# Six scatter groups in place of seven, a denser scatter of the first two, and zero rows written late, in an attention and mixture-of-experts kernel

## What is computed

```python
def reference(x, condB_zX, condB_zY, condB_zR, ...):
    ...
        logits = hn2 @ router_w.T
        rp = jax.nn.softmax(logits, axis=-1)
        topw, topi = jax.lax.top_k(rp, K)
        gates = jnp.sum(jax.nn.one_hot(topi, E, dtype=hn2.dtype) * topw[..., None], axis=1)
        hmid = jax.nn.gelu(jnp.einsum('th,ehf->tef', hn2, w1), approximate=False)
        y = jnp.einsum('tef,efh->th', hmid * gates[:, :, None], w2)
        return x1 + y.reshape(s, b, h)
    x = x + _L0_ffn_ref(_L0_cond_ref(x, ...), ...)
    return x
```

## The kernel before, in words

| iteration | slots before | slots after | steps scattered before | steps scattered after |
|---|---|---|---|---|
| 10, 11, 12 | none | none | 0 1, 2 3, 4 | none |
| 13 | -1 | none | none | 0 1 2 3 |
| 14 | none | none | 5 6 | 4 5 6 7 |
| 15 | none | -1, 0, 1 | 7 8 | none |
| 16 | 0, 1 | 2, 3, 4 | none | none |
| 17 | 2, 3 | 5 | none | 8 9 10 11 |
| 18 | 4, 5 | 6, 7 | 9 10 | none |
| 19 | 6, 7 | 8, 9 | 11 12 | none |
| 20, 21 | 8, 9 | 10, 11 | none | none, 12 13 |
| 22, 23, 24 | 10 to 15 | 12 to 17 | none, 13 14, 15 16 | 14 15, none, none |
| 25 | none | 18 | 17 | none |
| 26 | 16, 17 | 19, 20 | none | 16 17 |
| 27 | 18, 19 | 21 | none | 18 19 |
| 28 | 20, 21 | none | 18 19 | 20 |
| 29, 30 | 22 to 25 | 22 to 25 | 20 21, 22 | none |
| 31 to 34 | 26 to 30 | 26 to 30 | 23 to 26 in 32 and 33 | 21 to 25 |

## Time and profile before

### The profile page before, as it was taken

One profiled execution on the slowest core, in us unless ns is written; L12 is line 12 of the kernel. 1 busy time (PEld: TensorE's weight loads), 2 busy tenths in 40 slices (PEclk: granted clock), 3 DMA queues, 4 the chain that ended last, 5 costly groups with the idle time before them and its releaser, 6 DMA issues. The chain is left out here.

```text
span 723.5 us, 10160 instructions
## 1 busy us (share of the span) xinstructions
PE 585.2 (81%) x2640; PEld 405.8 (56%) x2640; DVE 434.1 (60%) x1028; ACT 349.0 (48%) x814; POOL 461.3 (64%) x562
## 2 busy tenths in 40 slices
PE   2567786764567969769999699999699999999992
PEld 1334454442346646546666466766477676676761
DVE  1256679974999998755895699989844000111110
ACT  4334443322433645527766456666257555444440
POOL 5787678688668565675778874584475854343432
PEclk9779997876888989889999699999899999999997
DMA  4377854233111321342324422243344544444332
GB/s 126 124 223 229 254 145 104 53 82 96 45 52 38 82 38 23 74 91 50 59 39 89 110 30 38 38 95 56 53 77 82 118 83 67 68 61 73 62 58 23
DMA packets 51547, 59.83 MB, mean 83 GB/s; under 512 B 7386, under 2 KB 47075, under 8 KB 51428
## 3 DMA queue, kind: packets, MB, share of 16 engines
q0 software_dynamic: 18288, 23.28, 20.2%
q1 hardware_dynamic: 33204, 35.91, 17.5%
HBM read 35.89 MB, written 27.46 MB: 88 GB/s over the span
## 5 line engine op out<-in xcount | busy, mean ns | idle before, releaser
L979 PE MATMUL b_y<-w_s,hm_hmT 128*128 x568 | 137.0, 385 | 11.8 <-ACT y L548 11.0
L446 POOL DMA_INDIRECT out_dram<-y,xin x71 | 117.9, 1660 | 34.0 <-issue 27.0
L964 PE MATMUL b_h<-w_s,xT 128*128 x284 | 134.4, 596 | 1.6 <-ACT xT L509 1.6
L979 PEld LDWEIGHTS b_y<-w_s,hm_hmT 128*128 128x128 f32 x568 | 103.5, 192 | 25.9 <-issue 14.6
L1116 PE MATMUL b_at<-ident,pv_prod 128*128 128x128 f32 x544 | 76.3, 291 | 25.8 <-DVE pv_prod L910 25.8
L681 DVE TENSOR_SCALAR y<-b_y,xin,live 128x256 f32<-128x256 f32 x24 | 13.1, 544 | 136.9 <-PE b_y L979 136.9
L910 DVE TENSOR_TENSOR pv_prod<-kv,pr 128x1024 f32<-128x1024 f32 (+2 forms) x80 | 82.6, 1074 | 19.8 <-PE b_at L1116 19.7
L844 DVE TENSOR_TENSOR qk_prod<-q,kv 128x1024 f32<-128x1024 f32 (+2 forms) x80 | 89.5, 1143 | 2.7 <-ACT kv L578 1.8
L1116 PEld LDWEIGHTS b_at<-ident,pv_prod 128*128 128x128 f32 x544 | 67.6, 154 | 30.0 <-issue 24.2
L414 POOL DMA_INDIRECT xs_d<-ring,slot_row x64 | 71.5, 1118 | 19.1 <-issue 18.2
L852 DVE TENSOR_REDUCE sc<-qk_prod 128x64 f32<-128x1024 f32 (+2 forms) x80 | 82.2, 1052 | 0.3
(11 more groups left out here) (168 smaller groups left out, 1038.1 us busy)
## 6 DMA issues: line engine op xcount, KB each, us to landing
xin<-xs_d SPq DMA_DIRECT2D x71, 132.5 KB, 2.2
w_s<-in_L_ffn_w_dram SPq DMA_DIRECT2D x16, 512.0 KB, 4.5
xp<-in_x_dram SPq DMA_DIRECT2D x32, 128.0 KB
xud<-in_x_dram SPq DMA_DIRECT2D x32, 128.0 KB
out_dram<-x POOLq DMA_DIRECT2D x32, 128.0 KB, 3.3
xud<-in_x_dram SPq DMA_DIRECT2D x32, 126.0 KB
out_dram<-y,xin POOLq DMA_INDIRECT x71, 3.9
xud<-in_x_dram SPq DMA_DIRECT2D x64, 1.0 KB
```

The lines of the kernel that those rows point to most:

```text
L446: pool.indirect_dma_start(out_rows, bass.IndirectOffsetOnAxis(ap=xin[:, j % NX, H:H + 1].bitcast(U32), axis=0), y[:, j % NY, :], None, com ...
L964: mm = pe.matmul(b_h[:, :], xT[:, k * P:(k + 1) * P], w1_s[:, bass.ds(e * (HC * F) + k * F, F)], start=(k == 0), stop=(k == HC - 1))
L979: mm = pe.matmul(b_y[:, 0:H], hmT[:, k * P:(k + 1) * P], w2_s[:, bass.ds(e * (FC * H) + k * H, H)], start=(k == 0), stop=(k == FC - 1))
```

## The change

Seven groups become six, with ends at steps 8, 12, 16, 21, 26 and 32. The first two groups are scattered four steps an iteration (one at the start, three at the end of GpSimd's iteration). `WANT` gives three slots to iterations 15 and 16, and other numbers to 17, 25, 27 and 28. The ring of normalised steps has 15 places in place of 16. The zero rows come from `xp`, which nothing uses any more after iteration 26, and are written two experts an iteration in iterations 27, 28, 30 and 31; the first tile of the last group waits for them.

```diff
--- before.py
+++ after.py
@@ -34,7 +34,7 @@
     ORDER = [(c, p) for a, b in ((0, FEW), (FEW, S)) for c in range(B // P) for p in range(a, b)]
     AGAIN = S + FEW
     KV = S + FEW
-    ENDS = (5, 9, 13, 18, 23, 27, G)
+    ENDS = (8, 12, 16, 21, 26, G)
     GROUPS = [range(a, b) for a, b in zip((0,) + ENDS, ENDS)]
     NG = len(GROUPS)
     GMAX = max(len(r) for r in GROUPS)
@@ -43,7 +43,7 @@
     TMAX = max(b - a for a, b in zip(FIRST, FIRST[1:]))
     CAP = G * P + 2 * P
     ROW = H + 1 + E
-    RING = 16
+    RING = 15
     NX = 6
     NY = 4
     SCALE = float(D) ** -0.5
@@ -135,7 +135,7 @@
         live = sb("live", [P, TMAX])
 
         xin = sb("xin", [P, NX, ROW])
-        zrow = xin[:, NX - 1, :]
+        zrow = xp[:, :, :].rearrange("p i h -> p (i h)")[:, 0:ROW]
         y = sb("y", [P, NY, H])
         xT = sb("xT", [P, HC * P])
         hm_hmT = sb("hm_hmT", [P, 2 * F])
@@ -181,16 +181,18 @@
         NPLACES = 2 + S // TP
         ROUTE = {GROUPS[r][-1] + 4: r for r in range(NG - 1)}
 
-        PER = 2
+        PER = [4, 4] + [2] * (NG - 2)
         SCATTER = {}
         for g, r in ROUTE.items():
             for i, step in enumerate(GROUPS[r]):
-                SCATTER[g + 2 + i // PER, i % PER] = step
+                SCATTER[g + 2 + i // PER[r], i % PER[r]] = step
+
+        PREFIX = (G - AHEAD - 1, G - AHEAD, G - 2, G - 1)
 
         PLACES = {0: (), 1: (0,), 2: (0, 1), 3: (0, 1, 2), 4: (0, 0, 1, 2)}
         LATER = {1: (2,), 2: (3, 4), 3: (2, 3, 4)}
 
-        WANT = [0] * 13 + [2] * 7 + [1] * 2 + [2] * 10 + [1] * 3
+        WANT = [0] * 13 + [3] * 4 + [2] * 3 + [1] * 2 + [2] * 3 + [1, 2, 1, 0] + [2] * 3 + [1] * 3
 
         def group_of(j):
             return [r for r in range(NG) if j >= FIRST[r]][-1]
@@ -300,7 +302,7 @@
                     r = group_of(j)
                     sp.wait_ge(s["tab_ready"], r + 1)
                     sp.wait_ge(scattered[r], 32 * len(GROUPS[r]))
-                if j == NX - 1:
+                if j == TAIL:
                     sp.wait_ge(s["pre_done"], 16 * E)
                 if j >= NX:
                     sp.wait_ge(*added_to(j - NX))
@@ -377,9 +379,7 @@
                 links_of.append(pool.iota(iota_w[:, :].rearrange("p (a b) -> p a b", b=2), [[16, ALL // 2 + 1], [0, 2]],
                                           base=0, channel_multiplier=0))
                 link(links_of[-1])
-                link(pool.memset(zrow, 0.0))
-                pool.tensor_copy(iota_f[:, :], iota_i[:, :])
-                pool.tensor_copy(zrow[:, H:H + 1].bitcast(I32), idt[:, 0:1]).then_inc(s["const_ready"], 1)
+                pool.tensor_copy(iota_f[:, :], iota_i[:, :]).then_inc(s["const_ready"], 1)
 
             def neighbours(g):
 
@@ -414,10 +414,13 @@
                     pool.indirect_dma_start(xs_d, bass.IndirectOffsetOnAxis(ap=slot_row[:, k, g:g + 1], axis=0),
                                             ring[:, g % RING, :], None).then_inc(scattered[r], 16)
 
-            def prefix():
-
-                pool.wait_ge(s["pre_ready"], 1)
-                for e in range(E):
+            def prefix(i):
+
+                if i == 0:
+                    link(pool.memset(zrow, 0.0))
+                    link(pool.tensor_copy(zrow[:, H:H + 1].bitcast(I32), idt[:, 0:1]))
+                    pool.wait_ge(s["pre_ready"], 1)
+                for e in (2 * i, 2 * i + 1):
                     pool.indirect_dma_start(xs_d, bass.IndirectOffsetOnAxis(ap=pre_row[:, e:e + 1], axis=0),
                                             zrow, None).then_inc(s["pre_done"], 16)
 
@@ -472,9 +475,10 @@
                     diffuse(g + AHEAD + 1)
                 for j in adds[1:]:
                     add_y(j)
-                if g == list(ROUTE)[0] + 3:
-                    prefix()
-                scatter_at(g, 1)
+                if g in PREFIX:
+                    prefix(PREFIX.index(g))
+                for n in range(1, max(PER)):
+                    scatter_at(g, n)
             left = [j - 1 for j in done_in(G + 2)] + list(range(LEFT[0] - 1, ALL))
             while left[0] < LEFT[1]:
                 add_y(left.pop(0))
```

## The result

The changed kernel takes 741.44 us (median of 4 runs, 739.84 to 741.80), the kernel before 724.88 on the same chip: the ratio is 1.0236, with a 95% interval of 1.0215 to 1.0256. The profiled execution spans 739.4 us for 723.5, so the spans differ by 15.9 and the medians by 16.6. The forecast sum was -13.1. The step from one to the other, 29 us, has to be found.

The account below looks back on a forecast made before the run. No single bound in the loop: VectorE early, GpSimd's DMAs in iteration 12, TensorE and VectorE in turns from 16; TensorE behind the loop. Window gains and costs summed to -13.1 from 724.75, so 712 us, range 701 to 725.

Parts of the forecast that it names:

- The bill of the first clump: Window 14: VectorE waits for the deviation behind eight scatter DMAs on GpSimd, +5.2 us (bounds 0, +8).
- What was priced at 5 behind it: Iteration 15: TensorE waits 5 us, cold, for the first tile at slot -1; window 15 becomes 29.0, +12.2 us.
- +1.5 in window 18 (bounds 0, +8): Window 18: GpSimd's six scatters behind two adds end 30 us into window 17; VectorE wants it at 28.3.
- Window 19, "-4.0": Iteration 19: adds due over a longer time free the result buffer TensorE waited 3.79 us for; -4.0 (bounds 0, -6).
- it keeps its length: Behind the loop: 40 slots before and after, TensorE always busy, so this part's time does not change.
- The zero rows, "+0.5 (bounds 0, +3)": Iterations 27 to 31: two zero-row DMAs each, 2.6 us, on a GpSimd with little to do; +0.5 us in all.
- 21 to 24 (+3.7) and 25 (+2.2): Windows 21 to 24 lose a routing beside full TensorE, -1.0; window 25 gains a slot and routing, +0.7 (bounds 0, +5).
- the slower one: Rival: GpSimd's queue becomes the bound from iteration 13 to 18; six windows take 147 us, total 732; chance 0.12.
- Cheap clumps: Rival: bunched scatters cost less, window 14 1 longer and window 15 needing 23.5; total 702 us; chance 0.17.
- The clock's case: Rival: iterations without slots lower TensorE's clock; half of 29 and 15 at 1.2 GHz add 4 and 7: 723; chance 0.07.

Follow-up runs that it names:

- the square: Four six-group kernels, scattered four or two steps an iteration, with three slots in some iterations or two at most: spans 739.4, 724.1, 730.0, 715.6 us.
- the last kernel: Changed kernel with all groups scattered by two, at most two slots, step 25 scattered last, four experts' zero rows each in 29 and 30: 712.65 us.

## Why the prediction was wrong

**Right.** One routing less and the zero rows out of iteration 12 gave 18.4 us in windows 9 to 13, where the sum had 20.4: without the eight DMAs alone window 12 is 9.0 us shorter, where the sum took off the whole wait of 11.31. The bill of the first clump was right in size and in place: VectorE waited 5.57 us for the deviation in window 14, where 5.2 was forecast (its own figures, 23.8 less 18.8, give 5.0). What was priced at 5 behind it, TensorE's wait for the first tile, was 8.94, and since it began earlier the window came out at 28.83 for 29.0. Windows 16, 17, 20, 27, 30 and 31 are each within 1.4.

**The step that failed is "+1.5 in window 18 (bounds 0, +8)".** It measured +13.7, beyond the upper bound. The term counted two adds, a wait for a landing and six scatters, put their end at 30 us after the start of window 17 and compared that with VectorE's need at 28.3. In the trace the last scatter ended at 284.03, 29.4 after that start, so the count was right. But an add, the neighbours and the deviations themselves come after it, up to 289.35. I had added 3.3 us for such a tail in window 14 and nothing for these 5.3; and everyone else who waits for that queue is missing. (1) Tile j is loaded when the result of tile j - 6 is added; a third slot in 15 and 16 makes this bind, since the adds come an iteration later, one landing apart. TensorE lost 3.93 us. (2) That load stands in SyncE's queue ahead of the loads of `x`; with no slot in 18 and its scatters spread, the window was still 7 us longer than before, from this and from the late adds (which of the two weighs how much wasn't separated). (3) Tile 9 is the first of its group and needs the scatters landed: 7.44 us. On top of the waits, TensorE's busy time grew by 3.8 us at the lower clock. I had written for iteration 15 that a group's first tile waits for its scatter and its load, and did not write it again for iteration 18, where it is just as true.

**Window 19, "-4.0".** It was to lose the wait for a result buffer because adds would be due over a longer time. The wait stayed, 4.07 us. Neither the third slots nor the clumps make it: it is 4.55 us with two slots and the clumps, 4.57 with two slots and no clumps, and 3.26 to 3.79 in the kernels with seven groups. Only the kernel with three slots in 17, 18 and 19 has it not, where TensorE stood 9.48 us for a tile in that window. What would remove it, no run shows.

**Behind the loop, "it keeps its length": +6.2.** I looked at the number of slots and at TensorE, which was full in the stretch read the earlier trace rows, but that began at 558.62, 22 us behind the start of window 33. Ahead of it are the last steps' deviations. Five scattered steps and the rows of 31 now stand before the last one in GpSimd's queue, where three steps did, and they have less time to pass, since window 31 without its routing takes 9.19 us for 15.87. The last deviation is ready 8.7 us after the start of window 33 (554.98), where it was 3.9 (540.53). TensorE waits 4.78 us for the step, where in the kernel before it waited 1.06:

```profile
542.09 0.44 PE L1079 MATMUL b_tr<-ident,ring 128*128 128x128 f32 x2 [1.06 <-DVE ring L672]
```

In the first 12 us of this part its granted clock is 0.78, where it was 1.00, and over the whole part it is busy for 2.3 us more. The kernel before with two experts' rows in 30 and in 31 kept its 186.9, so the rows cost here only where the queue was already late. Moving step 25 alone gave 3.0 of the 6.2 back, moving the rows of 30 and 31 alone 2.4, moving step 25 and the rows of 31 together 5.7 (192.5 to 186.8). With both moved the term "it keeps its length" holds, six steps in the last group and all.

**The zero rows, "+0.5 (bounds 0, +3)".** In the changed kernel window 28 took 2.9 more with them than with them behind the loop, but 28 and 29 together only 0.7; with the second group scattered by two, 28 and 29 together took 2.5 more. With the 2.4 that they cost behind window 32, they come to 3.1 to 4.9, at the upper bound or over it. GpSimd's share of busy time in an iteration says little of it: four experts' rows in 27 were free where 27 scattered nothing; where it scattered two steps they cost 5.2 more than two experts' there and two in 28.

**Not settled:** 21 to 24 (+3.7) and 25 (+2.2). Window 22 takes 19.36 us in the changed kernel and 16.2 to 16.4 in those with other slots in 18 or other scatters of the second group. But it also took 17.01 with step 25 moved, which touches nothing there, so that its 3 us follow from window 18 is likely and not shown. Window 25 has a routing, a slot and a clock of 0.77; it took 20.8 to 21.8 in three others with these groups (one slot in 18, two slots with and without clumps), which have two slots there. All are inside the bounds given, and no run takes it apart.

**The rivals.** The one that came nearest is the slower one, that GpSimd's queue becomes the bound from 13 to 18, at 732 us and a chance of 0.12. Its mechanism, waits for landings added to a queue in order, is what the runs show; the three-slot iterations, which it took for two adds more, are the larger half. Its size was too large there and its place too small: windows 13 to 18 took 138.0 us, where it had 147 and the forecast 126.7, and the rest of the way to 741 lies in windows 19 to 29 and behind the loop, where it added nothing. I argued against it with the deviations alone ("wanted 5 us after they can be made"), and again forgot the tiles. Cheap clumps is refuted by window 14 in both columns of the square. The clock's case did not come where it was placed: with the zero rows elsewhere, iteration 28, without a slot, took 15.27 at a clock of 0.78, 29 ran at 1.00, and 15 came out as forecast. A lower clock did cost 3.8 us in window 18 and some behind window 32, where waits had come first. That the last kernel, 712.65, meets the forecast of 712 is luck: its slots, scatters and zero rows stand elsewhere.

## What to carry to other kernels

When work is bunched in an in-order queue, list for each instruction behind it everyone who waits: the buffer that it frees, the load that stands behind another load in a second queue, and the first reader of what it writes. A wait priced once at a group's start comes again at the next group's start. And where a part "keeps its length", read its first microseconds as well as its middle; a free place in a queue is one where nothing else of that kind stands in the same iteration, not one where the engine's busy share is low. And measure the cheapest part of a change by itself: here moving the zero rows in the kernel before gave all that the best of the larger changes gave.

## What the runs showed of the hardware

An add to the output held GpSimd for 1.5 to 1.7 us (in the changed kernel up to 3.1 for some beside VectorE's products), and in a row they started 4.5 to 4.7 us apart (290.30, 294.93, 299.39), so three results took 10.6 us of the queue, from the start of the first to the end of the last, in iterations that last 17 to 20. The Trainium skill, DMA: Bandwidth & Descriptors, section Rules for kernel authors, says that an accumulating DMA reads its destination and writes it later with nothing held in between, and that one must wait for the earlier DMA's semaphore. The kernel's wait is that rule, and the 2.9 to 3.0 us of idle time ahead of each add are what it costs here.

The same elementwise instruction over 128 by 256 numbers took GpSimd 0.73 us, or 1.6, or 2.52, by what VectorE did beside it. In window 17 line 397 took 2.52 (263.05) beside a product of VectorE (line 848, from 262.73), line 398 took 0.73 (265.65) mostly beside a reduction (line 856), and line 399 took 1.60 (266.46) beside the next product. The Trainium skill, GPSIMD Engine Reference, section Key points, says that GpSimd shares its SBUF interfaces with VectorE and contends with instructions of it that have two SBUF inputs. The trace agrees: these products have two, and in window 18, while VectorE idled, the additions took 0.72 each (291.13 and 291.94).

A scatter held GpSimd for 0.97 us and 0.30 to the next, but 1.92 and 1.95 for the two at 274.75 and 276.98, which ran beside VectorE's products:

```profile
274.59 3.48 DVE L914 TENSOR_TENSOR pv_prod<-kv,pr 128x1024 f32<-128x1024 f32 x3
```

Standing right behind an add does not slow a scatter by itself: one behind an add in the kernel before took 1.00 (521.00). In the whole trace of the changed kernel, 53 of the 72 scatters and zero-row DMAs overlap no such product (lines 848 and 914), and none of them took over 1.12 us; the nine that took over 1.3 are all among the 19 that do overlap one. In the kernel before it is 44 with none over 1.18, and eleven over 1.3 among 28. This is read from the traces, and no experiment took the products away.
